# Half masks during the projection, PSUM emptied by ScalarE, and the adjacency's rows loaded from GpSimd's queue

## What is computed

```
seq    = (x @ W_seq).reshape(N, H, DH)              # N 2048, H 16, DH 32
score1 = einsum('nhd,d->hn', seq, a1);  score2 = einsum('nhd,d->hn', seq, a2)
scores = leaky_relu(score1[:, :, None] + score2[:, None, :], 0.2)
scores = scores + (1 - adj)[None] * (-65500)
hidden = einsum('hij,jhd->ihd', softmax(scores), seq).reshape(N, 512) @ W_out + b_out
out    = layernorm(x + elu(hidden))
```

## Time and profile before

| | |
|---|---|
| median of 3 runs | 540.7 us |
| profiled execution, whole | 539.98 us |
| its span in the profile | 537.9 us |
| mean granted TensorE clock | 0.988 |
| busy: PE, DVE, ACT, POOL | 94%, 88%, 84%, 6% |
| projection | from 12.6 to 85.6 us |
| head 0, first to last mask product | 91.4 to 118.5 us |

### The profile page before, as it was taken

How to read it: one execution, slowest core, us unless ns; L and a number is a source line. 1 busy time by engine, 2 the same in 40 slices (tenths; PEclk the granted TensorE clock), 3 DMA queues, 4 the chain that set the end, 5 groups by cost and what they waited for, 6 DMA issues and landing times.

```text
span 537.9 us, 15193 instructions
## 1 busy us (share of the span) xinstructions
PE 505.4 (94%) x6717; PEld 457.5 (85%) x6717; DVE 474.4 (88%) x714; ACT 451.0 (84%) x458; POOL 31.7 (6%) x64
## 2 busy tenths in 40 slices
PE   6999997679999999999999999999999999999993
PEld 5777785679999999999999999999999999744542
DVE  4465678998999989999999999999999899888886
ACT  2678698889998999999999999999998869356664
POOL 2000000000000000000000000000000000024542
PEclk9999998899999999999999999999999999999997
DMA  7999991220202202020120102202022040014443
GB/s 268 364 335 361 324 284 20 89 74 8 80 2 81 79 2 81 2 80 21 62 80 2 80 2 80 80 1 80 2 81 80 1 138 4 1 60 139 134 136 119
DMA packets 30433, 52.75 MB, mean 98 GB/s; under 512 B 18336, under 2 KB 19616, under 8 KB 26400
## 3 DMA queue, kind: packets, MB, share of 16 engines
q1 hardware_dynamic: 29824, 51.26, 28.8%
q10 hardware_dynamic: 544, 0.52, 0.3%
HBM read 43.25 MB, written 4.33 MB: 88 GB/s over the span
## 4 chain that ended last, share of the span: by engine, by line
PE 66%; ACT 16%; DVE 10%; DMA 5%; issue 2%; SPq 1%; POOLq 0%; POOL 0%; DVEq 0%; ACTq 0%
PE sums L414 31%; PE bank L430 17%; ACT tring L537 11%; PE sums L481 10%; PE sums L341 5%; DMA Vp<-tring 4%; DVE tring L829 3%; ACT low L579 1%; DVE tring L705 1%; DVE Vp L770 1%; PE bank L469 1%; ACT Vp L558 1%; DVE xp L764 1%; DMA abc<-in_x_dram 1%; ACT tring L507 1%
## 5 line engine op out<-in xcount | busy, mean ns | idle before, releaser
L537 ACT ACTIVATE tring<-abc,ab 128x2048 int8<-128x2048 f32 (+1 forms) x160 | 310.0, 2015 | 0.0
L414 PE MATMUL sums<-Vp,tring 128*128 128x132 f16 x4096 | 245.8, 222 | 13.4 <-DVE tring L829 8.1
L414 PEld LDWEIGHTS sums<-Vp,tring 128*128 128x128 fp8e4 x4096 | 239.8, 98 | 16.8 <-DVE tring L829 8.7
L829 DVE TENSOR_TENSOR tring<-adj,tring 128x512 uint32<-128x512 uint32 x256 | 166.8, 684 | 10.2 <-ACT tring L537 10.0
L430 PE MATMUL bank<-Vp,adj 128*128 128x132 f16 x2048 | 126.1, 221 | 0.7 <-DVE Vp L770 0.7
L705 DVE TENSOR_SCALAR tring<-abc,ab 128x2048 int8<-128x2048 f32 (+1 forms) x98 | 124.3, 1268 | 0.0
L430 PEld LDWEIGHTS bank<-Vp,adj 128*128 128x128 fp8e4 x2048 | 122.1, 96 | 1.3 <-DVE Vp L770 1.1
L341 PE MATMUL sums<-Vp,abc 128*128 128x272 f32 x256 | 63.6, 402 | 3.5 <-DVE acc L688 2.8
L341 PEld LDWEIGHTS sums<-Vp,abc 128*128 128x128 f32 x256 | 48.4, 195 | 13.5 <-ACT abc L496 3.7
L481 PE MATMUL sums<-abc,Vp 128*128 128x512 f32 (+1 forms) x136 | 57.5, 568 | 0.3 <-ACT Vp L624 0.3
L481 PEld LDWEIGHTS sums<-abc,Vp 128*128 128x128 f32 x136 | 24.7, 190 | 22.9 <-issue 22.0
(11 more groups left out here) (90 smaller groups left out, 287.7 us busy)
## 6 DMA issues: line engine op xcount, KB each, us to landing
Vp<-in_adj_dram SPq DMA_DIRECT2D x16, 1024.0 KB, 7.8
abc<-a_rows SPq DMA_DIRECT2D x15, 1024.0 KB, 4.7
abc<-in_x_dram SPq DMA_DIRECT2D x16, 256.0 KB, 5.5
Vp<-in_x_dram SPq DMA_DIRECT2D x16, 256.0 KB, 3.0
out_dram<-Vp SPq DMA_DIRECT2D x16, 256.0 KB, 2.1
abc<-in_L_gnn_W_out_dram SPq DMA_DIRECT2D x1, 1024.0 KB, 5.3
Vp<-in_L_gnn_W_seq_dram ACTq DMA_DIRECT2D x2, 256.0 KB, 3.3
Vp<-in_L_gnn_W_seq_dram SPq DMA_DIRECT2D x2, 256.0 KB, 4.7
```

The source lines that it names most:

```text
L414: mm = pe.matmul(bank[b][:, c * 2 * VW:(c + 1) * 2 * VW], slot(jt)[:, it * P:(it + 1) * P].bitcast(F8), Vp[:, h, jt, :, :], start=(jt == 0 ...
L537: return act.activation(slot(jt)[:, columns], row(h)[:, columns], ACT.Sign, bias=ab[:, jt, H + h:H + h + 1], scale=-1.0)
L829: dve.tensor_tensor(words, adj8[:, jt, :].bitcast(U32), words, ALU.bitwise_and).then_inc(t_ready, 1)
```

## The change

1. *ACT empties PSUM.* `copy_ab` and `copy_seq` move from DVE to ACT; DVE takes the magnitudes from the copy in SBUF (`magnitudes`), except for the last tile.
2. *Casts one tile later, adjacency copies on DVE.* ACT's cast of tile t comes in its round t+1; of the 16 adjacency copies DVE makes 14 and ACT 2 (12 and 13), four after the projection. Before, each made 8.
3. *Half masks.* For 9 of head 0's 16 tiles the first 1024 columns are compared (6 on DVE, 3 on ACT) and ANDed in the projection's rounds 9 to 14 or right behind it. PE multiplies these halves first (`EARLY`), then the second halves and the last 7 whole tiles. `DVE_TILES[0]` becomes (1, 3, 4, 6, 7, 8), so that ACT makes tiles 9 to 15.
4. *Row 0* of the scores is spread in rounds 4, 8 and 12 instead of around the last two projections, into banks 6 and 7.
5. *The start.* `a2` is loaded by ACT's queue, the blocks of `W_seq` for DVE and GpSimd are 0 and 2, and PE gets fillers, matmuls whose result nobody reads (`warm`): 14 before the first work, 5 and 4 and 4 in the start, 5 and 5 and 24 in the change-over.
6. *The adjacency's loads* are issued by GpSimd instead of SP: two before its products of `W_seq`, 14 behind them, each from the fifth on when the cast of the tile four before is done.

```
-BY_PE = (2, 3)
+BY_PE, BY_VECTOR = (1, 3), (0, 2)
...
-DVE_TILES = (SIX, SIX, SEVEN, ...
+DVE_TILES = ((1, 3, 4, 6, 7, 8), SIX, SEVEN, ...
+EARLY = 9
+FIRST, SECOND, WHOLE = slice(0, N // 2), slice(N // 2, N), slice(0, N)
+DVE_EARLY = {9: (1,), 10: (3, 4), 11: (6,), 12: (7,), 13: (8,)}
+ACT_EARLY = {10: 0, 11: 2, 13: 5}
+AND_EARLY = {11: (0,), 12: (1,), 13: (2,), 14: (3, 4, 5)}
...
+def mask_columns(h, jt):
+    return SECOND if h == 0 and jt < EARLY else WHOLE
...
 # SP
             for t in range(NT):
-                load_adj(t)
-                if t >= STAGE - 1:
-                    turn_adj(t - STAGE + 1)
+                if t >= STAGE:
+                    turn_adj(t - STAGE)
                 if t + XS - 2 < NT:
                     load_x(t + XS - 2)
...
 # PE
+            def warm(n):
+                for _ in range(n):
+                    pe.matmul(bank[2][:, 0:2 * P], ones16[:, 0:P], ones16, start=True, stop=True)
...
+            for t in range(1, NT):
+                if t + 1 < NT:
+                    turn_x(t + 1)
+                else:
+                    spread_row0(3, range(12, 14))
                 project(t).then_inc(seq_made, 1)
+                if t in (4, 8, 12):
+                    spread_row0(t // 4 - 1, range(t - 4, t))
...
+                if h == 0:
+                    for jt in range(EARLY):
+                        if jt == PARTS[1].start:
+                            pe.wait_ge(v_ready, 2)
+                        pe.wait_ge(t_first, jt + 1)
+                        mask_products(h, jt, range(NT // 2))
...
 # ACT
+            for t in range(NT):
+                if 0 < t < NT - 1:
                     copy_x(t + 1)
+                if t >= 1:
+                    copy_ab(t - 1)
+                    copy_seq(t - 1)
+                    cast_adj(t - 1)
+                if t in (5, 9, 13):
+                    copy_row0(t // 4 - 1)
+                if t in ACT_EARLY:
+                    jt = ACT_EARLY[t]
...
+                    sign(0, jt, FIRST).then_inc(u_first, 1)
+            cast_adj(NT - 1)
+            copy_row0(3)
+            copy_seq(NT - 1)
...
+            factors(0, slice(0, 1))
+            split_high(0, PARTS[0])
+            copy_adj(NT - 4)
+            split_high(0, PARTS[1])
+            copy_adj(NT - 3)
...
 # DVE
             for t in range(NT):
+                if t >= 2:
+                    fix_adj(t - 2)
+                if t >= 4:
+                    copy_adj(t - 4)
+                for jt in DVE_EARLY.get(t, ()):
...
+                    above_row(0, jt, FIRST).then_inc(above_first, 1)
+                for jt in AND_EARLY.get(t, ()):
+                    join_first(jt)
+                if t >= 1:
+                    dve.wait_ge(seq_copied, t)
+                    magnitudes(t - 1, seq[:, t - 1, :, 0:DH].rearrange("p (s h) d -> p s h d", s=2))
...
             values(0, PARTS[0])
+            join_first(7)
+            split_low(0, PARTS[0])
+            values(0, PARTS[1])
+            join_first(8)
+            copy_adj(NT - 2)
+            split_low(0, PARTS[1])
+            copy_adj(NT - 1)
...
 # GpSimd
+            def load_adj(t):
+                if t >= STAGE:
+                    pool.wait_ge(adj_cast, t - STAGE + 1)
+                pool.dma_start(stage[:, t % STAGE, :], adj_n[t // 2, t % 2]).then_inc(adj_loaded[t % STAGE], 16)
+            for t in range(2):
+                load_adj(t)
             pool.wait_ge(a12_copied, 2)
...
+            for t in range(2, NT):
+                load_adj(t)
```

More of the change, by code:

```diff
@@ L253, in load_x @@
                 sp.dma_start(xs[:, t % XS, :], x_t(t)).then_inc(x_loaded[t % XS], 16)
[L255 to L263, removed]
+            load_a(sp, 0, a1)
             load_x(0)
-            for k in range(1, KT, 2):
+            for k in range(0, KT, 2):
                 load_w(sp, k)
@@ L360, in spread_row0 @@
             def spread_row0(c, tiles):
+                pe.wait_ge(ab_copied, tiles[-1] + 1)
+                if c >= 2:
+                    pe.wait_ge(row0_copied, c - 1)
                 for t in tiles:
@@ L367, in _ @@
             pe.wait_ge(ones_set, 1)
+            warm(14)
             pe.wait_ge(a12_loaded, 32)
@@ L372, in _ @@
             mm.then_inc(a_spread, 1)
+            warm(5)
+            pe.wait_ge(ident, 1)
             turn_x(0)
@@ L375, in _ @@
             turn_w(1)
+            warm(4)
             pe.wait_ge(block_ready, 1)
@@ L407, in _ @@
             mm.then_inc(a_turned, 1)
-            pe.wait_ge(row0_copied, 4)
+            warm(24)
             pe.wait_ge(seq_copied, NT)
@@ L487, in _ @@
         def _(act):
-            for k in range(0, KT, 2):
+            load_a(act, 1, a2)
+            for k in range(1, KT, 2):
                 load_w(act, k)
@@ L516, in copy_row0, with copy_wa @@
                 act.copy(row(0)[:, c * 512:(c + 1) * 512], row0_bank[c]).then_inc(row0_copied, 1)
+            def copy_wa(n):
+                act.wait_ge(wa_made, n + 1)
+                act.copy(Wx[:, BY_PE[n], :, half:WC], wa_bank(n)).then_inc(wa_copied, 1)
             copy_x(0)
@@ L658, in _ @@
             dve.wait_ge(a12_copied, 2)
-            for k in range(BY_PE[0]):
+            for n, k in enumerate(BY_VECTOR):
                 dve.wait_ge(w_loaded[k], 16)
@@ new lines, in _ @@
+            largest(3, slice(NT - 4, NT - 1))
+            dve.wait_ge(mx_part, 8)
+            dve.tensor_reduce(most, mxc.rearrange("p c k -> p k c"), AX.X, ALU.max).then_inc(most_ready, 1)
+            fix_adj(NT - 2)
+            dve.wait_ge(seq_made, NT)
+            dve.tensor_copy(ab[:, NT - 1, :].rearrange("p (s h) -> p s h", s=2), projected(NT - 1, slice(half, WC))).then_inc(ab_copied, 1)
+            magnitudes(NT - 1, projected(NT - 1, slice(0, half)).rearrange("p s (h d) -> p s h d", d=DH))
@@ L827, in _ @@
                         dve.wait_ge(u_ready, act_count(h, jt))
-                    words = slot(jt).bitcast(U32)
-                    dve.tensor_tensor(words, adj8[:, jt, :].bitcast(U32), words, ALU.bitwise_and).then_inc(t_ready, 1)
+                    join_adj(jt, mask_columns(h, jt)).then_inc(t_ready, 1)
                     if h == 0 and jt == 0:
-                        split_low(0, PARTS[0])
-                    if h == 0 and jt == 1:
-                        values(0, PARTS[1])
                         dve.wait_ge(Mb_ready, 1)
@@ L840, in _ @@
                         dve.wait_ge(scales_set, 2)
-                    if h == 0 and jt == 3:
+                    if h == 0 and jt == 4:
                         dve.wait_ge(a_turned, 1)
```

190 lines of the change are left out of this document (83 added, 107 removed).

## The result

The changed kernel takes 575.9 us, the median of four runs, against 540.8 for the kernel before beside it: slower, ratio 1.0506 (1.0465 to 1.0547), about 27 us. The forecast was 539.1 in a range of 535.8 to 546.5. Throughout, a ratio leaves out the runs that are over 1.5% longer than the shortest of their kernel (here two of four, which is why the medians differ by 35 us), and a median doesn't. The profiled execution of the changed kernel, 580.3 us, is one of its longer ones; the shortest took 564.2.

The account below looks back on a forecast made before the run. DMA and PE were taken to limit the projection nearly alike, mask makers the end of head 0. 78.0 + 37.4 = 115.4, plus 1.6 lateness: 117.0, -1.5; 539.98 became 538.5, plus 0.7 about 539.1 us, range 535.8 to 546.5.

Parts of the forecast that it names:

- Loads on GpSimd: Adjacency loads on GpSimd's empty queue during the projection: issue cost hidden by three to four rounds, 3 to 7 us to spare.
- The first rival: Loads crowd out transposes at the DMA engines, weights land late and DVE stops: +1 to +8 us, say 544; chance 0.20.
- GpSimd's descriptors: Rival: DVE's work keeps GpSimd from issuing loads in time; at 0.3 us a tile +3.3 net, 544; chance 0.07.
- Start: Up to tile 0 made: fillers raise PE's clock, `a2` on another queue saves an issue; -4.0 us, tile 0 at 14.5.
- Projection: Tile 0 to the projection's end: PE no longer waits for DVE; 61.7 + 1.8 us, ending at 78.0, -7.6.
- T: End of head 0's projection: 85.6 us before, 78.0 forecast.
- Tail: From the projection's end to the end of head 0: 37.4 us, 4.5 more than before.
- ACT's two waits: In the tail ACT waits for DVE: about 2.4 us for the row factors, 2.0 for the second `values`.
- Lateness: Last transposes and DVE's lag, as DMA demand per tile exceeds PE's: 0 to 3 us on top, 1.6 taken.
- E: End of head 0: 118.5 us before, 117.0 forecast, -1.5.

## Why the prediction was wrong

*The failed step is "Loads on GpSimd"*, in its last clause: "if loads and transposes share fairly". The sum of DMA work there (70 to 74 us against 77) took for granted that the engines move what they moved before, 340 GB/s, whatever queues the work stands in. They didn't: 183 and 155 GB/s, at shares of 1.38 and 1.24, and the twelfth transpose, which the sum had done by 74 us, was issued at 108. I priced two queues as a question of order only, and never of how much gets through.

*The first rival had the mechanism in part and its price wrong.* It named the late `W_seq`, DVE stopping and its fixes falling behind, and the condition (a transpose landing over 8.2 us after its issue). It gave +1 to +8, since it let each transpose take 3.0 us once its turn came. The last five did; the five before them landed after 11.2 to 30.3 us. Measured +27 by the ratio, +35 by the medians. A misreading lies beneath: the 12.74 us for four transposes, taken for time at the head of SP's queue, hold 4.6 us of waits for DVE's fixes. (The last sum of the forecast also gives 539.2, not 539.1.)

*Its first half holds.* At the start the pieces do take turns. Queues in 5 to 10 us of the changed kernel (packets, MB, share), q0 being GpSimd's, q10 ScalarE's:

```profile
q0 software_dynamic: 199, 1.51, 77.4%
q10 hardware_dynamic: 200, 0.20, 11.8%
q1 hardware_dynamic: 159, 0.16, 10.1%
```

Nearly one piece of 8 KB for each of 1 KB: 80% of the bytes go to the loads that nobody needs yet, and `W_seq` lands after 12 us. I had "no earlier than 17.5" for tile 0; it was 26.3. The Trainium skill's rule (DMA: Bandwidth & Descriptors, Queues, rings and completion order), turns "at *packet* granularity", is in keeping with these counts; a packet there can hold several pieces, and the counts don't say how many a turn takes. One for one is no rule for every size: beside the same loads 5 pieces of SP's queue went for one of GpSimd's in 75 to 100 us of the changed kernel (2538 to 526), and 7 with ordinary DMAs (4865 to 701). For the transposes such turns don't suffice either: the kernel with ordinary DMAs has pieces of the same 256 B and moves 346 GB/s.

*What the break-down is.* Shown: it takes transposing DMAs (with ordinary ones of the same size neither trace has any), in flight together with loads of another queue (kept apart, in one run: none). It comes whether that queue is ScalarE's or GpSimd's. With one load there at a time there is none. With loads and transposes in one queue there is none either, though several loads are issued and not yet landed there too (the median load lands after 8.2 us, and one goes out every 4 to 5). In the break-down a piece of SP's queue takes some five times as long. Not shown: what happens in the DMA engines then. Open too: whether the depth of the other queue or the demand sets it off, why smaller pieces don't help, what decides between a long and a short run, and the 6 us that a second queue costs with ordinary DMAs.

*GpSimd's descriptors* (0.07): fell. ScalarE's queue does the same harm, and an issue takes GpSimd 0.53 us.

*The other steps held in the main*, as the kernel with loads on SP's queue shows. Start: forecast -4.0, tile 0 at 14.5; measured -2.4, at 16.2. The weight transposes saved nothing (2.16 us for 8, 2.22 before; 1.1 forecast), the 8-column products 1.6 (1.85 after 3.42; 1.7 forecast) and the first projection its 1.9. The first weight transpose stands 0.2 later than before (7.47 and 7.27), where 0.7 was to be won by `a2`'s queue, and the two groups of fillers behind it cost 0.9 (1.4 forecast for all three groups). Projection: forecast T - tile 0 = 63.5, measured 62.8 (79.0 - 16.2). Tail: forecast 37.4, measured 117.8 - 79.0 = 38.8, with ACT's two waits at 2.88 and 2.00 for 2.4 and 2.0. Lateness: 1.6 forecast on top of both; DVE waited 1.4 us for transposes after 60 us, within the tail and the projection as measured. E: 117.0 forecast, 117.8 measured; the time 539.1, and 539.3 measured. That the sum comes out so near is in part luck: the start fell short by 1.6, the tail by 1.4, and 0.7 in the projection and the 1.6 of lateness made up for most of it. But the change without its title's last clause does what I forecast, and the clause was priced at nothing.

## What to carry to other kernels

Before moving transfers to a second queue, ask what else is in flight: a queue is not only an order, it is also a share. Loads that nobody needs yet took 80% of the bytes from weights that everyone waited for, and loads beside transposing DMAs of another queue halved what all of them got through. Keep transposing DMAs and bulk loads in one queue, in the order in which they are needed, and read the DMA share and the GB/s together: a share over 1 at half the usual rate means that transfers hinder each other. And where the runs of one kernel spread over 20 us, as here, four of them can't show what 8 us at the start are worth; that takes more runs, or a change that removes the spread first.

## What the runs showed of the hardware

- Pieces of 8 KB and of 1 KB in three queues went about one for one: 199 of 8 KB, 200 and 159 of 1 KB in 5 us. It isn't so for every size: beside pieces of 8 KB, 5 to 7 times as many small ones (256 B, and some of 2 KB) of another queue went. With 2 KB pieces in the third queue the 1 KB pieces' DMAs land after 9 us instead of 12.
- Transposing DMAs (256 KB) in one queue and two or more 1 MB loads in another: landings up to 31.9 us, 124 to 183 GB/s at shares over 1 for 10 to 20 us, against 3.0 to 9.2 us with all in one queue. A small piece then takes 0.112 us, with ordinary DMAs in its place 0.023 (estimates from the queues' shares). Alone they land after 3.0 to 3.6, beside a single load of another queue 3.0 to 5.3.
- The extra time varies from run to run: 541.8 to 567.4 us for one and the same kernel with half of the loads in each queue.
